# Attention parts stored one by one and loaded in long rows; query rows gathered by number

## The reference

```
h  = tokens(x, value)                  # 4000 gathered embedding rows + value * w + b, normalised
h += ssm(norm(h))                      # long convolution over the sequence, gelu
h += moe8(norm(h))                     # 8 experts 128-512-128, the best 2 of each token
h += sampled_attention(norm(h))
h += moe64(norm(h))                    # 8 groups x 8 experts 128-256-128, the best 2 x 2
```

```
q, k, v = x Wq' + bq, x Wk' + bk, x Wv' + bv      # per head
Ks      = k at 2560 sampled positions
QKs     = q Ks' / 4
M       = max(QKs) - mean(QKs)                    # per query
U       = argmax over the 500 queries of M        # one query per batch and head: 64 numbers
a       = softmax(q[U] k' / 4)                    # 64 rows of 500
h      += (a v) Wo' + bo                          # the same row for every token of a batch
```

## Time and profile before

| | us |
|---|---|
| median of 3 runs | 1270.65 |
| profiled execution | 1269.81 |
| span of its records | 1267.9 |
| PE busy | 779.4 (61%) |
| DVE busy | 766.9 (60%) |
| POOL busy | 599.8 (47%) |
| ACT busy | 416.4 (33%) |

### The profile page before, as it was taken

One profiled execution on the slowest core, in us unless ns is written; L12 is line 12 of the kernel. 1 busy time (PEld: TensorE's weight loads), 2 busy tenths in 40 slices (PEclk: granted clock), 3 DMA queues, 4 the chain that ended last, 5 costly groups with the idle time before them and its releaser, 6 DMA issues.

```text
span 1267.9 us, 18789 instructions
## 1 busy us (share of the span) xinstructions
PE 779.4 (61%) x4781; PEld 616.3 (49%) x4782; DVE 766.9 (60%) x2219; ACT 416.4 (33%) x1127; POOL 599.8 (47%) x619
## 2 busy tenths in 40 slices
PE   0106963979999267788677601569999997541000
PEld 0105453779999134344255500358888886431000
DVE  6994275746666348878741599956666665533332
ACT  2354151614444324333001500844445453210000
POOL 8862000355552636652100000567777775377776
PEclk9657975569999556656556565569999999855555
DMA  2390069012222295686400120414344459522222
GB/s 68 119 375 1 1 187 349 3 39 68 68 73 52 58 157 96 119 125 95 73 1 0 44 83 5 132 45 105 102 102 105 106 89 74 65 61 69 61 69 60
DMA packets 116910, 111.06 MB, mean 88 GB/s; under 512 B 16779, under 2 KB 103690, under 8 KB 116618
## 3 DMA queue, kind: packets, MB, share of 16 engines
q1 hardware_dynamic: 101252, 78.56, 24.3%
q0 software_dynamic: 15616, 32.01, 13.8%
HBM read 81.03 MB, written 29.46 MB: 87 GB/s over the span
## 4 chain that ended last, share of the span: by engine, by line
PE 44%; DVE 26%; DMA 9%; POOL 9%; issue 5%; ACT 4%; SPq 2%; DVEq 0%; POOLq 0%; ACTq 0%
PE ps L512 12%; PE ps L506 11%; POOL zbuf L730 7%; DVE zbuf L1093 5%; DMA zbuf<-xrows,holder 3%; DVE bnst L778 3%; DVE zbuf L1002 3%; DMA zbuf<-results,place 3%; PE ps L1568 3%; PE ps L502 2%; PE ps L1678 2%; PE ps L1596 2%; DMA big<-parts 2%; PE ps L1719 2%; ACT xbuf L1371 2%
## 5 line engine op out<-in xcount | busy, mean ns | idle before, releaser
L709 POOL DMA_INDIRECT zbuf<-xrows,holder x264 | 254.5, 964 | 140.4 <-PE ps L502 87.6
L730 POOL DMA_INDIRECT zbuf<-results,place x192 | 185.7, 967 | 90.1 <-issue 51.1
L512 PE MATMUL ps<-big,zbuf 128*128 x1328 | 205.4, 287 | 19.7 <-ACT zbuf L474 11.4
L506 PE MATMUL ps<-zbuf,tbuf 128*128 128x128 f32 x1340 | 203.0, 284 | 2.0 <-DVE zbuf L433 2.0
L512 PEld LDWEIGHTS ps<-big,zbuf 128*128 128x128 f32 x1328 | 170.9, 194 | 30.6 <-issue 28.4
L506 PEld LDWEIGHTS ps<-zbuf,tbuf 128*128 128x128 f32 x1340 | 174.4, 196 | 5.8 <-DVE zbuf L433 1.7
L1093 DVE TENSOR_REDUCE zbuf<-ps 125x3 f32<-125x1500 f32 (+1 forms) x96 | 143.2, 1540 | 45.7 <-PE ps L1568 45.0
L474 ACT ACTIVATE zbuf<-ps,tbuf 128x128 f32<-128x128 f32 x335 | 115.0, 365 | 154.0 <-PE ps L506 153.4
L433 DVE COPY zbuf<-ps 128x128 f32<-128x128 f32 x264 | 76.9, 291 | 139.0 <-PE ps L506 134.9
L1568 PE MATMUL ps<-big 97*125 97x500 bf16 x256 | 110.4, 575 | 51.0 <-DVE zbuf L1093 31.1
L1072 DVE SCALAR_TENSOR_TENSOR h<-zbuf,gate,h 125x128 f32<-125x128 f32 x152 | 52.8, 352 | 123.6 <-DMA zbuf<-results,place 121.8
(11 more groups left out here) (355 smaller groups left out, 1163.5 us busy)
## 6 DMA issues: line engine op xcount, KB each, us to landing
results<-zbuf SPq DMA_DIRECT2D x130, 128.0 KB, 1.8
big<-kappa SPq DMA_DIRECT2D x8, 1750.0 KB, 20.8
big<-parts SPq DMA_DIRECT2D x96, 125.0 KB, 6.2
big<-in_L_ffn_W_dram SPq DMA_DIRECT2D x10, 1024.0 KB, 9.1
big<-in_L_ffn_W_dram SPq DMA_DIRECT2D x64, 128.0 KB, 2.7
parts<-zbuf SPq DMA_DIRECT2D x8, 750.0 KB, 4.5
zbuf<-xrows,holder POOLq DMA_INDIRECT x264, 2.6
xrows<-xbuf SPq DMA_DIRECT2D x2, 1792.0 KB
```

The lines of the kernel that those rows point to most:

```text
L506: last = t.matmul(ps[:, (2 if k < c.HC // 2 else 4) + u % 2, 128 * k:128 * k + 128], ring.w1[u % U][:, 128 * k:128 * k + 128], ring.rT[u % ...
L512: last = t.matmul(ps[:, 6 + u % 2, 0:D], ring.hid[u % 2][:, 128 * k:128 * k + 128], w2v[:, bass.ds(e, 1), k, :].rearrange("p e d -> p (e d ...
L709: gp.indirect_dma_start(ring.rows[tau % RING], None, xrows[:, :], bass.IndirectOffsetOnAxis(ap=holder[:, tau:tau + 1], axis=0)).then_inc(S ...
L730: gp.indirect_dma_start(got[n % 8], None, results[f][:, :], bass.IndirectOffsetOnAxis(ap=place[f][:, k, t:t + 1], axis=0)).then_inc(S(f"go ...
```

## The change

The parts are stored part by part. Each has two transfers, one for queries and one for keys, issued when that part is ready. In DRAM a part now lies as [feature within the head][head][token], so that the eight heads of a feature are one row of 8000 bytes. The stack's groups are put in another order (queries 2, 0, 1, 1, 0, 0 and keys 0, 0, 0, 1, 1, 2 in place of 0, 0, 0, 1, 1, 2 and 0, 1, 2, 0, 1, 0), so that a load can fill 16, 32 or 48 rows of the stack with copies of one part: three loads for part 0, two for part 1, two for part 2. The source of such a load is written with the number of copies as its first dimension, with step 0. The same six products are made.

The x of each batch is also stored to DRAM (`xattn`, as [token][128]), behind the batch's loads on SP. In place of the comparison, its transposes and the first `rows_times`, DVE adds the place and the first row number of the batch, POOL gathers the 64 rows of `xattn` by number, and PE turns them once. DVE prepares the row numbers of the batches (`batch_row`) during the attention's preparations, ahead of the first expert block; POOL writes the counts for them earlier.

```diff
+        xattn = nc.dram_tensor("xattn", (B * L, D), F32)
...
-        q_parts, k_parts = (0, 0, 0, 1, 1, 2), (0, 1, 2, 0, 1, 0)
+        part_rows = ((0, 1, 1), (0, 4, 2), (1, 0, 3)), ((0, 2, 2), (1, 3, 2)), ((0, 0, 1), (1, 5, 1))
...
+            def store_part(b, n, ready):
+                sp.wait_ge(S(ready), b + 1)
+                for w in range(2):
+                    sp.dma_start(ap(parts_d, (b * 6 + w * 3 + n) * D * L, [[L, H], [H * L, DK], [1, L]]),
+                                 parts[:, w, n, :]).then_inc(S(f"part{n + 1}_st"), 16)
+
+            def load_part(b, n):
+                sp.wait_ge(S(f"part{n + 1}_st"), 32 * (b + 1))
+                for w, g, copies in part_rows[n]:
+                    sp.dma_start(stack[DK * g:DK * (g + copies), w, b % 2].rearrange("p h t -> p (h t)"),
+                                 ap(parts_d, (b * 6 + w * 3 + n) * D * L, [[0, copies], [H * L, DK], [1, H * L]])
+                                 ).then_inc(S(f"stack{b % 2}"), 16)
+
             for b in range(B):
-                sp.wait_ge(S("parts_ready"), b + 1)
-                sp.dma_start(ap(parts_d, b * 6 * D * L, [[L, D], [D * L, 6], [1, L]]),
-                             parts.rearrange("p w n t -> p (w n) t")).then_inc(S("parts_st"), 16)
-                sp.wait_ge(S("parts_st"), 16 * (b + 1))
+                store_part(b, 0, "part1_ready")
+                store_part(b, 1, "part2_ready")
                 if b >= 2:
                     sp.wait_ge(S("scores_filled"), len(GROUPS) * (b - 1))
-                for w, order in enumerate((q_parts, k_parts)):
-                    for g, n in enumerate(order):
-                        sp.dma_start(stack[DK * g:DK * g + DK, w, b % 2],
-                                     ap(parts_d, (b * 6 + w * 3 + n) * D * L, [[L, DK], [DK * L, H], [1, L]])
-                                     ).then_inc(S(f"stack{b % 2}"), 16)
+                load_part(b, 0)
+                store_part(b, 2, "parts_ready")
+                load_part(b, 1)
+                load_part(b, 2)
+                sp.dma_start(ap(xattn, b * L * D, [[D, R], [R * D, J], [1, D]]), x[:, J * b:J * b + J, :]).then_inc(S("xa_st"), 16)
...
+            me.did(gp.iota(batch_row.bitcast(I32), pattern=[[0, 1]], base=0, channel_multiplier=1))
...
+                    pool.wait_ge(S("chosen_ready"), 1)
+                    pool.wait_ge(S("xa_st"), 16 * B)
+                    gp.indirect_dma_start(picked, None, xattn[:, :], bass.IndirectOffsetOnAxis(ap=chosen, axis=0)
+                                          ).then_inc(S("chosen_in"), 16)
...
+                me.then(v.tensor_copy(batch_row, batch_row.bitcast(I32)))
+                me.then(TS(batch_row, batch_row, (H - 1) / 2.0, 1.0 / H, ALU.subtract, ALU.mult))
+                me.then(TS(batch_row, batch_row, MAGIC, None, ALU.add))
+                me.did(TS(batch_row, batch_row, MAGIC, float(L), ALU.subtract, ALU.mult))
...
-                TS(hot, i500[0:64, :], i8f, None, ALU.is_equal).then_inc(S("hot_ready"), 1)
-                wait_bank(dve, "hotT")
-                emptied(v.tensor_copy(hotT, bank(at["hotT", 0])[0:R, 0:256].rearrange("p (j n) -> p j n", j=J)))
+                TS(chosen, i8f, batch_row, None, ALU.add).then_inc(S("chosen_ready"), 1)
...
-                            act.wait_ge(S("parts_st"), 16 * b)
+                            for n in range(3):
+                                act.wait_ge(S(f"part{n + 1}_st"), 32 * b)
...
-                    pe.wait_ge(S(f"stack{b % 2}"), 16 * 12 * (b // 2 + 1))
+                    pe.wait_ge(S(f"stack{b % 2}"), 16 * 7 * (b // 2 + 1))
...
-                pe.wait_ge(S("hot_ready"), 1)
-                p = use("hotT")
-                for j in range(J):
-                    last = t.transpose(p[0:R, 64 * j:64 * j + 64], hot[:, R * j:R * j + R], ident[0:64, 0:64])
-                filled(last)
...
-                wait_evac(pe, "hotT")
-                filled(rows_times(use("xsel"), hotT))
+                pe.wait_ge(S("chosen_in"), 16)
+                p = use("xsel")
+                filled(t.transpose(p[:, 0:64], picked, ident[0:64, 0:64]))
```

More of the change, by code:

```diff
@@ L120, in bank_plan @@
             plan += [("wT", 0, "dve"), ("cols", 0, "dve"), ("cnt", 0, "dve"), ("cntrow", 0, "dve")]
-            plan += [(w, 0, "dve") for w in ("MT", "hotT", "xsel", "qsel", "u")] + [("ss", 0, "act")]
+            plan += [(w, 0, "dve") for w in ("MT", "xsel", "qsel", "u")] + [("ss", 0, "act")]
             plan += [(w, 0, "dve") for w in ("attT", "xa", "ctx")] + [("outa", i, "dve") for i in range(2)]
@@ L300, in tower_kernel @@
         xbar = take(B)
-        q_parts, k_parts = (0, 0, 0, 1, 1, 2), (0, 1, 2, 0, 1, 0)
+        batch_row, chosen = take(1, 64), take(1, 64).bitcast(I32)
+        part_rows = ((0, 1, 1), (0, 4, 2), (1, 0, 3)), ((0, 2, 2), (1, 3, 2)), ((0, 0, 1), (1, 5, 1))
         SROWS = 6 * DK + 1
@@ L309, in tower_kernel @@
         mrow = zbuf[0:64, 256:256 + L]
-        hot = zbuf[0:64, 768:768 + L]
-        hotT = zbuf[0:R, 1280:1280 + 256].rearrange("p (j n) -> p j n", j=J)
+        picked = zbuf[0:64, 768:896]
         xsel = zbuf[:, 1536:1600]
```

## The result

The changed kernel takes 1321.31 us (median of four runs, 1319.23 to 1322.83) where the kernel before takes 1271.2 us on the same chip: a ratio of 1.0396, with a 95% interval of 1.0377 to 1.0416. It is 50.1 us slower; the prediction said 1317 us, 46.4 slower. The profiled execution took 1321.48 us with a span of 1319.8.

A forecast was written before the change was run, and what follows sets the result against it. The first DMA engine's queue, 30.6 us a batch against 22.95 without waits, was taken as the bound: 1269.8 + 57.3 (stage) - 11.6 (gather) + 0.8 (preparation) = 1316.3, with 0.8 for the median 1317; range 1295 to 1345.

The forecast's parts named there:

- The loads run on 2 or 3 engines, always the same: Attention loads: four multi-copy loads share one first engine, which carries 67 rows of 8000 B, 21.4 us a batch.
- Rival A: Attention loads: dealt over all engines, or different ones each time, so no batch waits; 1243 us, chance 0.16.
- C: Attention loads: an engine reading 8 KB rows alone is slower than in a crowd, 6.7 us a batch; 1371, chance 0.07.
- The rest of the queue: First engine, per batch: part stores, x store, gathers and a gap join the loads' 21.4 us; sum 30.9, used as 30.6.
- (d): First engine's queue: the first load waits for a store of its own batch to land, engine idle; 0.8 us a batch.
- (a): First engine's queue: six part stores with head count outermost run on 8 engines instead of 16; 4.4 us a batch.
- (c): First engine's queue: eight gathers of 64 KB, one share each; 1.3 us a batch.
- Batch 0: Start of the attention stage: first matmul of scores moves from 461.2 to 467.7, 6.5 us later.
- The gather: Query rows after the attention maxima: an add, a gather and a transpose take 4.4 us instead of 16.0; 11.6 saved.
- Rival D: Query-row gather: it waits for the queue of x stores and loses its gain; +11.6, 1329, chance 0.02 within the forecast's.
- Preparation: Before the attention stage: four small DVE operations ahead of the one PE waits for; +0.8 us.
- Rival B: Attention stage: loads confined, but stores of parts run on all engines, 2.2 us less per batch; 1302, chance 0.12.

The follow-up runs named there:

- e1: Changed kernel with each load of 2 or 3 copies written as single-copy loads, twelve in all; 1341.91 us, 0.9898 of the kernel before.
- e11: Changed kernel with nine copy-free loads, three taking two different parts, the parts 64 elements further apart in DRAM; 1384.35 us, 1.0217 of the kernel before.
- e7: Kernel before, only that each load's 16 rows lie on every sixth partition; 1336.2 us, 0.9934 of the kernel before.
- e3: Changed kernel's stores and loads of parts, without the x store and the gather; 1404.78 us, 1.0349 of the kernel before.
- e10: Changed kernel with each batch's x store split into 112 and 13 partitions; 1311.24 us, 1.0326 of the kernel before.
- e8: Changed kernel with one store per part and twelve loads of 1000 B rows onto every sixth partition; 1320.82 us, 0.9807 of the kernel before.
- e4: Kernel before with the x store and gather added, its old single store and 12 loads kept; 1341.33 us, 0.9883 of the kernel before.

## Why the prediction was right, step by step

**The loads run on 2 or 3 engines, always the same: shown.** The step that carried the forecast. The share of 0.13 is two engines; e1 takes the loss away by the copy count alone; e11 makes it again with a real step. That they are the same engines is seen in batch 3, whose four such loads are issued from 541.07 to 546.33. Windows of the changed kernel:

```profile
546.00:549.00 3.00, 2.81 (x12) 2.58 (x13) 2.80 (x3) 0.62 (x2) 0.00 (x0) 0.50 0.19 80
551.00:553.00 2.00, 1.66 (x6) 1.16 (x5) 2.00 (x2) 0.53 (x2) 0.00 (x0) 0.50 0.13 53
```

0.19 x 16 is 3 engines, then 2; on different engines the four loads would have kept up to 9 busy at once. That they are the first ones by number is not in the records, neither for these loads nor for the 125 rows of the output store. 67 rows at 0.302 us are 20.2 us where 21.4 was forecast. The Trainium skill's rule on a leading copy count ("DMA: Bandwidth & Descriptors", Rules for kernel authors) is borne out by the trace, with 2 engines for 2 copies. Rival A, all engines (1243), is refuted, and so is C: an engine alone is faster than in the crowd, not slower. What C read from the earlier trace rows, 131 ns for a row of 1000 B, was the crowding of 16 partitions: on average a row of 1000 B takes 0.100 us in the kernel before and 0.054 in e7 (packets of 470 to 690 us, stores included).

**The rest of the queue.** Forecast 30.9 us a batch, measured 31.5. The terms by the packets of batch 3 (540.5 to 571.9 us): 96 rows of 1000 B at 0.051 us are 4.9, where 4.4 was said; 100 rows of x at 0.030 are the 3.0 of the forecast, though leaving them out gained only 2.1 (e3); eight gathers put a packet of 4096 B and 0.26 us each on an engine, 2.1 and not 1.3. With 20.2 for the loads that is 30.2, and 1.3 us are left. Two things fill them. A single-copy row isn't 0.30 us everywhere: in batches 3 to 5 two of the sixteen rows of the first load take 0.9 to 1.0, the others 0.3 to 0.6, and they fit the engines that start last. And the gap (d), in which the first load waits for a store to land, put at 0.8, is hardly there: in batch 3 rows of a store are moving until the load begins at 541.62, and in batches 2 to 7 at most 0.3 us lie between the last row of that load and the first two-copy row. So (d) was too large and the rows (a), (c) and the single copies too small; that the sum fits to 0.6 us is in part luck. Packets of one engine can overlap, so none of this holds to the tenth. Timeline of SP in the changed kernel:

```profile
528.73 8.47 SPq L555 DMA_DIRECT2D parts<-zbuf  x4
540.71 1.79 SPq L561 DMA_DIRECT2D big<-parts  x3
542.54 1.30 SPq L555 DMA_DIRECT2D parts<-zbuf  x2
543.88 12.26 SPq L561 DMA_DIRECT2D big<-parts  x4
```

The four stores need 8.47 us only to be issued, and the loads go out 3.5 us behind them; the third part's store, issued at 542.54, stands in the queue behind three loads, and with the wait for it the last four loads take 12.26 us to issue. The forecast had put SP's 14 transfers "under the queue" at 0.4 us each. They take far longer than that, but the engines of the copies have rows to move meanwhile, so they are under it all the same.

**Batch 0: right in kind, too small.** PE's wait before its first matmul of scores was forecast to move from 461.2 to 467.7 and came to 473.98; 2.45 of these were there before the stage (the front starts at 432.68, before at 430.23; see Preparation), so it is 10.3 us where 6.5 was said. The prediction took 1.3 us for gathers; the packets of 13 lie between the first store and the first matmul (eight issued until 451.8, one each 1.25 us, five more from 465.93), and at 0.25 us of queue each they are 3.3. That is up to 2 us of the missing 3.8; the rest isn't accounted for. That ACT would wait for batch 0's third part came true with 10.40 us, and by the rhythm cost nothing more.

**The stage.** Forecast +57.3 us, measured +63.6 (270.5 - 206.9): 3.8 in batch 0 and 7 x 0.35 in the steps (473.98 to 690.62 is 7 x 30.95, against 30.6). The 20.9 us behind batch 7's first matmul held to the tenth (690.62 to 711.52).

**The gather.** Forecast -11.6, measured -12.6: it landed in 2.45 us where 3.3 was taken. Rival D, a gather that waits for the x stores, did not occur. TensorE's clock behind it: forecast 0, measured +0.1 (L1625 takes 8.74 us, L1610 took 8.66).

**Preparation.** Forecast +0.8. DVE's four operations take 0.7 us. The changed kernel was already 2.2 us late ahead of them (L1027 starts at 259.26, L1010 at 257.04 before), where DVE and PE have nothing new. e10 has the same preparations, and there the operation starts at 257.23 and the front at 430.45, 0.2 us after before's 430.23. So the 2.45 us belong to that execution and not to the change, and of the 0.8 at most 0.2 is seen.

**Rival B**, stores of the parts on all engines (1302), is refuted by the packet counts: 8 engines a store. The window at 443.0, a share of 0.54 with a gather beside the stores, fits. All told, +63.6 and +2.45 against 57.3 and 0.8, the gather's -12.6 against -11.6, and 1.5 us regained behind it in the later stages: +51.9 in the span, against +46.5.

## What to carry to other kernels

Write the large dimension of a transfer outermost, on both sides, and write copies as transfers of their own; fewer, longer transfers are no gain if each is dealt to two engines and all to the same two. To see it, multiply the DMA share in a window with one kind of transfer by 16. And where the share is near 1 with few GB/s, look at which partitions are filled: spreading 16 rows over 96 partitions was worth 9.2 us here (e7 against before; e8 against e4 is some 10 us by their ratios, with part-by-part stores besides), and the length of the rows nothing.

## What was not expected of the hardware

- Loads onto 16 neighbouring partitions moved 114 to 155 GB/s at a share near 1, and onto every sixth partition 185 to 224, at a lower share. In the kernel before, with its share of 0.93, this looked like a full DMA system and was a narrow target.
- A small store behind large loads on few engines lands late: 125 KB took up to 13.5 us (chain of waits of the changed kernel, start, us, what):

```profile
447.54 13.49 DMA parts<-zbuf
...
543.21 12.14 DMA parts<-zbuf
```

- The same kernel takes 6 to 7% longer on some chips, with the ratio of the change the same (1.0396 and 1.0393). On those PE stands 10 to 14 us longer ahead of batch 0; why stays open.
